# A recommendation tower: twenty embedding fields selected by one-hot matmuls, twelve gathered, in every unit

## The chip, the cores and the metric

One core of a Trainium2 chip. The metric is the device time of one execution in microseconds, for which the median of several runs is given; lower is better. A profile shows the span of one execution, a little less than its time.

## The reference, cut to what matters

2048 samples, 32 categorical fields. Each field has a table of 64 floats a row (14 tables of 1000 rows, 12 of 1250, 3 of 12500 and 3 of 125000), and each sample one row number per field.

```python
e = jnp.stack([tbl_0[ids[:, 0]], ..., tbl_31[ids[:, 31]]], axis=1)   # 2048 x 32 x 64
gram = jnp.einsum('bnd,bmd->bnm', e, e)
z = gram[:, rows, cols]                                              # the 496 pairs above the diagonal
h = jnp.concatenate([z, dense_ctx], axis=1)                          # 496 + 16 = 512
h = jnp.maximum(h @ W_top1 + b_top1, 0.0)                            # 512 -> 512
h = jnp.maximum(h @ W_top2 + b_top2, 0.0)                            # 512 -> 256
y = h @ W_top3                                                       # 256 -> 1
```

## The kernel before, in words

The batch is worked in four units of 512 samples; a unit has two rounds of 256. A row of a table reaches `vecs` (64 numbers of a field on partitions, samples and fields along them) in one of two ways.

*Gathered* fields: POOL issues one indirect DMA per field and 128 samples (`gather`, L289) into `rows`. PE transposes four fields at a time (`turn`, L502: four transposes into one half of `gat_ps`), ACT copies them to `vecs` (`gathered`, L326). The rows of a turn's slot are fetched for the next unit as soon as the turn has been made for this one: `gather(u, r, x)` waits for `gat_full` of unit u - 1. So POOL works only after turns.

*Selected* fields: the table stays in SBUF (`tabs`), split into three bf16 pieces that sum to the f32 value (ACT: `high`, `middle`; DVE: `rest` L425, `low` L430, once, during unit 0), as chunks of 125 rows: 8 chunks for 1000 rows, 10 for 1250. Two fields are a pair. SP spreads the pair's ids over all partitions (`load_wide`), DVE compares them with the row numbers (`one_hots`, L442: one instruction of 128x512 per chunk) into a ring of four pieces, PE multiplies (`select`, L487: chunks x 3 pieces x 2 fields matmuls, 48 for a pair of 8-chunk fields, 60 for 10-chunk ones), ACT copies (`selected`, L318, four copies of 64x256).

Then per round PE multiplies each sample's 32 vectors with themselves (`gram`, L517, 4 chunks of 128 small matmuls), ACT or DVE copies the products out, SP writes them to DRAM and reads them back as rows of pairs (`rows_out`, `rows_back`), and the three layers follow one unit late (L531, L540, L549), woven in between gram chunks.

PE's written order in unit u: `select(u, 2..)`, with turns of round 0 behind the later pairs; then gram of round 0 with `layer1(u-1, 0..3)`; then turns of round 1 with `select(u+1, 0)` and `select(u+1, 1)` among them; then layer 2 and 3 of u - 1 with the gram of round 1. ACT and SP have the same kind of written order. In unit 0 all gathers of both rounds are issued at once at the start.

Before the change there are 16 selected and 16 gathered fields in units 0 and 3; in units 1 and 2 (`SHIFTED`) the last pair, fields 30 and 31 (10 chunks), is gathered too, as a fifth turn of two fields. So pairs are 8, 7, 7, 8, turns per round 4, 5, 5, 4 and gathers 64, 72, 72, 64. `PAIRS`, `TURNS`, `units_with_pair`, `units_with_turn`, `turn_slots` and `turn_columns` keep account of that.

Of the kernel before, what the change touches and what calls it, by code (L numbers as in the profile page):

```python
# [13 lines left out]
P = 128  # L14
# [30 lines left out]

PAIRS = [ALL_PAIRS - (u in SHIFTED) for u in range(UNITS)]
TURNS = [ALL_TURNS - (u not in SHIFTED) for u in range(UNITS)]
PAIRS_TO = [sum(PAIRS[:u]) for u in range(UNITS + 1)]
MOST_PAIRS = max(PAIRS)
TURNS_TO = [ROUNDS * sum(TURNS[:u]) for u in range(UNITS + 1)]  # L50


def sel_no(u, g):
    return PAIRS_TO[u] + g


def gat_no(u, r, x):
    return TURNS_TO[u] + TURNS[u] * r + x


def units_with_pair(u, g):

    return sum(g < PAIRS[v] for v in range(u))


def units_with_turn(u, x):

    return sum(x < TURNS[v] for v in range(u))


def turn_slots(x):
    return slice(4 * x, min(4 * x + 4, N_ROWS))


def turn_columns(x):
    return slice(4 * x, 4 * x + 4) if 4 * x < N_GAT else slice(FIELDS - 2, FIELDS)

# [5 lines left out]
def piece_no(u, g, half, at):  # L83

    return 4 * (PAIRS_TO[u] + g) + 2 * half + at

# [6 lines left out]
def dlrm_tower_kernel(nc, chunks, ctx_t, ids_gat, ids_sel, tables, packed, w1, b1, w2, b2, w3, out):  # L93
    first_chunk = [sum(chunks[:k]) for k in range(N_SEL)]
    halves = [((0, c // 2), (c // 2, c)) for c in chunks]
    half_most = max(b - a for h in halves for a, b in h)
    pair_chunks = [(first_chunk[2 * g], chunks[2 * g] + chunks[2 * g + 1]) for g in range(ALL_PAIRS)]
    pair_most = max(k for _, k in pair_chunks)
    assert all(chunks[2 * g] == chunks[2 * g + 1] for g in range(ALL_PAIRS))

    with ExitStack() as ctx:
# [11 lines left out]
        gat_ids = sb("gat_ids", [P, UNITS * ROUNDS * 2 * N_ROWS], I32)  # L113
        sel_ids = sb("sel_ids", [P, N_SEL * BATCH // P], I32)
# [3 lines left out]
        onehot = sb("onehot", [P, RING, half_most, UNIT], BF16)  # L118
        rows = sb("rows", [P, ROUNDS, N_ROWS, 2, DIM], F32)
        vecs = sb("vecs", [P, HALF, FIELDS], F32)  # L120
# [39 lines left out]
        onehot_used = sem("onehot_used")  # L160
        rows_in = [[sem(f"rows_in{r}_{x}") for x in range(ALL_TURNS)] for r in range(ROUNDS)]
        sel_emptied = sem("sel_emptied")
# [17 lines left out]
        def _(sp):  # L180
# [7 lines left out]
            def load_wide(u, w):  # L188
                last = [v for v in range(u) if w < PAIRS[v]][-1:]
                for v in last:  # L190
                    sp.wait_ge(onehot_ready, piece_no(v, w, 1, 1) + 1)
# [38 lines left out]

            first = ROUNDS * 2 * N_ROWS
            sp.dma_start(gat_ids[:, 0:first], ids_gat[:, 0:first]).then_inc(gat_ids_in[0], 16)
# [7 lines left out]
            for w in range(N_SEL // WIDE):  # L240
                load_wide(0, w)
            for g in range(STAGE_SLOTS, MOST_PAIRS):
                load_stage(g)
# [5 lines left out]
            for u in range(LAST):  # L249
                for w in range(PAIRS[u + 1]):  # L250
# [23 lines left out]
        def _(pool):  # L274
# [8 lines left out]
            def gather(u, r, x):  # L283
                for v in [v for v in range(u) if x < TURNS[v]][-1:]:
                    pool.wait_ge(gat_full, gat_no(v, r, x) + 1)
                for k in range(N_ROWS)[turn_slots(x)]:
                    for h in range(2):
                        at = ((u * ROUNDS + r) * 2 + h) * N_ROWS + k
                        nc.gpsimd.indirect_dma_start(  # L289
                            out=rows[:, r, k, h, :], out_offset=None, in_=tables[ROWS_OF[k]],  # L290
                            in_offset=bass.IndirectOffsetOnAxis(ap=gat_ids[:, at:at + 1], axis=0))\
                          .then_inc(rows_in[r][x], 16)

            for u in range(UNITS):
                if u < 2:
                    pool.wait_ge(gat_ids_in[u], 16)
                for r in range(ROUNDS):
                    for x in range(TURNS[u]):
                        gather(u, r, x)

        @block.scalar
        def _(act):
# [19 lines left out]
            def gathered(u, r, x):  # L322
                n, at = gat_no(u, r, x), turn_columns(x)
                fields = at.stop - at.start
                act.wait_ge(gat_full, n + 1)
                nc.scalar.copy(vecs[:, P * r:P * r + P, at],  # L326
                               gat_ps[:, n % 2, 0:P * fields].rearrange("p (f j) -> p j f", f=fields))\
                  .then_inc(gat_emptied, 1)

# [45 lines left out]
            for u in range(UNITS):  # L375
                for g in range(2, PAIRS[u]):
                    selected(u, g)
                    if u == 0 and g + 4 < MOST_PAIRS:
                        high(g + 4)
                        middle(g + 4)  # L380
                    if g >= 4:
                        gathered(u, 0, g - 4)
                for x in range(PAIRS[u] - 4, TURNS[u]):
                    gathered(u, 0, x)
                if u == 0:
# [8 lines left out]
                gram(u, 0, 1, (0, 1))  # L394
                for x in range(TURNS[u]):
                    gathered(u, 1, x)
# [19 lines left out]
        def _(dve):  # L416
# [16 lines left out]
            def one_hots(u, g, half):  # L433
                if half == 0:
                    dve.wait_ge(wide_in[g], 16 * units_with_pair(u + 1, g))
                for at in range(2):
# [17 lines left out]
            rest(1)  # L454
            for g in range(MOST_PAIRS):
                one_hots(0, g, 0)
                if g + 1 < MOST_PAIRS:
                    low(g + 1)
                one_hots(0, g, 1)
                if g + 2 < MOST_PAIRS:  # L460
                    rest(g + 2)
            for u in range(1, UNITS):
                for g in range(PAIRS[u]):
# [8 lines left out]
        def _(pe):  # L472
# [22 lines left out]
            def turn(u, r, x):  # L495
                n = gat_no(u, r, x)
                if n >= 2:
                    pe.wait_ge(gat_emptied, n - 1)
                slots = range(N_ROWS)[turn_slots(x)]
                pe.wait_ge(rows_in[r][x], 16 * 2 * len(slots) * units_with_turn(u + 1, x))  # L500
                for at, k in enumerate(slots):
                    last = nc.tensor.transpose(gat_ps[:, n % 2, P * at:P * at + P],  # L502
                                               rows[:, r, k, :, :].rearrange("p h d -> p (h d)"), ident[:])
                last.then_inc(gat_full, 1)

            def gram(u, r, c):
                b = c // 2
                if c == 0:
                    pe.wait_ge(sel_emptied, PAIRS_TO[u + 1])
                    pe.wait_ge(gat_emptied, gat_no(u, r, TURNS[u] - 1) + 1)  # L510
                if c % 2 == 0 and emptied_no(u, r, b) > 0:
# [87 lines left out]
def laid_out(np, inputs):  # L599
# [18 lines left out]
    for f in SELECTED:  # L618
# [36 lines left out]
```

## Time and profile before

| | us |
|---|---|
| median of 3 runs | 666.53 (664.74 to 671.36) |
| the profiled execution | 669.14 |
| its span | 666.8 |
| PE busy (weight loads apart) | 405.4 (61%) |
| POOL busy | 267.0 (40%) |
| DVE busy | 165.0 (25%) |
| ACT busy | 142.3 (21%) |

PE is the tensor engine, PEld its weight loads, DVE the vector engine, ACT the scalar engine, POOL the engine that issues the gathers, SP the one that issues most other transfers. In a timeline the bracket is idle time ahead of the instructions and what ended it; "issue" is idle time for which the profile shows nothing awaited, "remote" one whose releaser it doesn't show. Neighbouring instructions of one kind are merged, with their count behind the x.

### The profile page before, as it was taken

The numbers are of one execution on the slowest core, as the hardware profiler recorded it, in microseconds if no ns is written. First come the engines' busy times: TensorE is split into PE (matmuls) and PEld (weight loads), VectorE is DVE, ScalarE is ACT, GpSimd is POOL, SyncE is SP. The second block draws the span as 40 slices with busy tenths as digits, with TensorE's granted clock in tenths as the row PEclk, the third lists the DMA queues.
The fourth block names the chain that finished last, engine by engine and source line by source line (L and its number), as shares of the span: only waits on it lengthen the run. The fifth ranks groups of instructions, "written<-read, shape, count | busy, mean of one in ns | idle before, by whom it ended". The sixth has DMA issues, their size and how long they took to land.

```text
span 666.8 us, 13226 instructions
## 1 busy us (share of the span) xinstructions
PE 405.4 (61%) x5956; PEld 212.2 (32%) x5956; DVE 165.0 (25%) x513; ACT 142.3 (21%) x232; POOL 267.0 (40%) x280
## 2 busy tenths in 40 slices
PE   0632138762664249641973657962793667999877
PEld 0200014321421135310530334521350234555455
DVE  4410049631022007410030203640011204720000
ACT  4020007411100033220110014340120014543111
POOL 6777700766176500675076610367047420000000
PEclk9855559955586559975995768976696669999898
DMA  8411123211011117511011004821001004501340
GB/s 274 136 28 26 28 87 131 54 22 25 9 27 23 21 27 146 148 26 22 3 25 24 17 9 74 212 61 27 6 16 26 15 12 74 114 1 20 78 93 0
DMA packets 39058, 36.08 MB, mean 54 GB/s; under 512 B 14870, under 2 KB 27992, under 8 KB 38875
## 3 DMA queue, kind: packets, MB, share of 16 engines
q1 hardware_dynamic: 29866, 25.14, 15.5%
q0 software_dynamic: 8704, 8.93, 6.8%
q8 instruction: 46, 0.75, 0.5%
q10 hardware_dynamic: 432, 1.18, 0.5%
q14 instruction: 10, 0.07, 0.0%
HBM read 27.15 MB, written 8.07 MB: 53 GB/s over the span
## 4 chain that ended last, share of the span: by engine, by line
PE 50%; issue 23%; another core or an unknown queue 13%; DVE 7%; ACT 4%; SPq 1%; DMA 1%; DVEq 0%; ACTq 0%
PE sel_ps L487 24%; PE tower_ps L531 9%; PE gram_ps L517 9%; PE tower_ps L540 5%; DVE onehot L442 4%; PE gat_ps L502 3%; ACT vecs L318 2%; PE tower_ps L549 1%; DVE work L425 1%; DVE tabs L430 1%; ACT work L335 1%; SPq L202 1%; ACT h L348 0%; DMA products<-work 0%
## 5 line engine op out<-in xcount | busy, mean ns | idle before, releaser
L289 POOL DMA_INDIRECT rows<-in_tbl_dram,gat_ids x272 | 266.1, 978 | 270.5 <-PE gat_ps L502 178.5
L487 PE MATMUL sel_ps<-onehot,tabs 128*64 128x512 bf16 x1464 | 212.9, 418 | 136.4 <-issue 83.1
L442 DVE TENSOR_SCALAR onehot<-ids_wide,row_ids 128x512 bf16<-128x512 f16 x488 | 141.0, 361 | 324.1 <-PE sel_ps L487 183.4
L487 PEld LDWEIGHTS sel_ps<-onehot,tabs 128*64 128x64 bf16 x1464 | 93.1, 118 | 248.5 <-issue 174.2
L517 PE MATMUL gram_ps<-vecs 64*32 64x32 f32 x4096 | 62.7, 215 | 106.2 <-issue 95.4
L318 ACT COPY vecs<-sel_ps 64x256 f32<-64x256 f32 x120 | 72.1, 601 | 100.1 <-PE sel_ps L487 58.5
L517 PEld LDWEIGHTS gram_ps<-vecs 64*32 64x32 f32 x4096 | 50.4, 116 | 133.1 <-issue 121.2
L531 PE MATMUL tower_ps<-work,w_sb 128*128 128x512 f32 (+1 forms) x160 | 67.9, 580 | 2.8 <-DMA work<-products 2.8
L531 PEld LDWEIGHTS tower_ps<-work,w_sb 128*128 128x128 f32 x160 | 34.0, 221 | 27.5 <-issue 21.2
L326 ACT COPY vecs<-gat_ps 128x512 f32<-128x512 f32 (+1 forms) x36 | 19.7, 567 | 107.3 <-remote 45.1
L449 DVE COPY work<-gram_ps 128x512 f32<-128x512 f32 x8 | 5.2, 687 | 135.4 <-PE gram_ps L517 135.4
L540 PE MATMUL tower_ps<-h,w_sb 128*128 128x512 f32 (+1 forms) x80 | 35.4, 596 | 1.1 <-ACT h L341 1.1
L341 ACT ACTIVATE h<-tower_ps,b_sb 128x512 f32<-128x512 f32 (+1 forms) x20 | 12.0, 602 | 96.8 <-PE tower_ps L531 78.0
L502 PE MATMUL gat_ps<-ident,rows 128*128 128x128 f32 x136 | 23.7, 311 | 11.0 <-issue 10.4
L311 ACT CAST tabs<-work 128x1024 bf16<-128x1024 f32 (+1 forms) x8 | 8.6, 1072 | 86.5 <-DVE work L425 65.5
L335 ACT COPY work<-gram_ps 128x512 f32<-128x512 f32 x24 | 13.0, 589 | 50.0 <-PE gram_ps L517 50.0
L502 PEld LDWEIGHTS gat_ps<-ident,rows 128*128 128x128 f32 x136 | 16.4, 156 | 21.8 <-issue 20.7
L540 PEld LDWEIGHTS tower_ps<-h,w_sb 128*128 128x128 f32 x80 | 17.1, 223 | 15.2 <-issue 12.4
L348 ACT ACTIVATE h<-tower_ps,b_sb 128x512 f32<-128x512 f32 (+1 forms) x10 | 5.5, 599 | 59.2 <-PE tower_ps L540 59.2
L425 DVE TENSOR_TENSOR work<-work,tabs 128x1024 f32<-128x1024 f32 (+1 forms) x8 | 10.1, 1262 | 4.3 <-issue 4.3
L430 DVE TENSOR_TENSOR tabs<-work,tabs 128x1024 bf16<-128x1024 f32 (+1 forms) x8 | 10.1, 1267 | 1.1 <-issue 1.1
L549 PE MATMUL tower_ps<-h,w_sb 128*1 128x512 f32 (+1 forms) x20 | 9.1, 582 | 1.9 <-ACT h L348 1.9
(12 smaller groups left out, 15.1 us busy)
## 6 DMA issues: line engine op xcount, KB each, us to landing
ids_wide<-ids_scratch SPq DMA_DIRECT2D x30, 256.0 KB
rows<-in_tbl_dram,gat_ids POOLq DMA_INDIRECT x272
products<-work SPq DMA_DIRECT2D x12, 248.0 KB, 4.2
products<-work SPq DMA_DIRECT2D x24, 120.0 KB, 4.5
work<-in_packed_dram SPq DMA_DIRECT2D x5, 512.0 KB
work<-products SPq DMA_DIRECT2D x9, 256.0 KB
work<-in_packed_dram ACTq DMA_DIRECT2D x2, 512.0 KB
w_sb<-in_w_dram SPq DMA_DIRECT2D x1, 1024.0 KB, 6.0
```

Source lines behind the costliest of these rows:

```text
L289: nc.gpsimd.indirect_dma_start(out=rows[:, r, k, h, :], out_offset=None, in_=tables[ROWS_OF[k]], in_offset=bass.IndirectOffsetOnAxis(ap=ga ...
L318: last = nc.scalar.copy(vecs[DIM * h:DIM * h + DIM, :, N_GAT + 2 * g + at], sel_ps[DIM * at:DIM * at + DIM, sel_no(u, g) % 2, HALF * h:HAL ...
L326: nc.scalar.copy(vecs[:, P * r:P * r + P, at], gat_ps[:, n % 2, 0:P * fields].rearrange("p (f j) -> p j f", f=fields))\
L335: nc.scalar.copy(gram_rows[:, r, h, :, 16 * b:16 * b + 16], gram_ps[:, h, :, :].rearrange("p i m -> p m i")).then_inc(gram_emptied, 1)
L425: nc.vector.tensor_tensor(piece, piece, tabs[:, c0:c0 + k, 0, :], ALU.subtract).then_inc(rest_ready, 1)
L430: nc.vector.tensor_tensor(tabs[:, c0:c0 + k, 2, :], stage[g % STAGE_SLOTS][:, 0:k, :], tabs[:, c0:c0 + k, 1, :], ALU.subtract).then_inc(ta ...
L442: last = nc.vector.tensor_scalar(onehot[:, n % RING, c - c0, :], ids_wide[:, k, :], row_ids[chunks[k]][:, c:c + 1], None, ALU.is_equal)
L487: last[at] = nc.tensor.matmul(sel_ps[DIM * at:DIM * at + DIM, n % 2, :], tabs[:, first_chunk[k] + c, part, :], onehot[:, piece_no(u, g, ha ...
L502: last = nc.tensor.transpose(gat_ps[:, n % 2, P * at:P * at + P], rows[:, r, k, :, :].rearrange("p h d -> p (h d)"), ident[:])
L517: last = nc.tensor.matmul(gram_ps[32 * s:32 * s + 32, h, i, :], v, v, start=True, stop=True, skip_group_check=True)
L531: last = nc.tensor.matmul(tower_ps[:, j % 2, 0:width], w1_sb[:, c, P * j:P * j + P], z[:, c, x0:x0 + width], start=(c == 0), stop=(c == Q ...
L540: last = nc.tensor.matmul(tower_ps[:, o, 0:width], w2_sb[:, j, P * o:P * o + P], h1[:, j, 0:width], start=(j == 0), stop=(j == J1 - 1), sk ...
```

## The change

Fields 16, 21, 23 and 29 (1250 rows each) join the selected ones. All units then have ten pairs (seven of 8 chunks, then three of 10) and three turns of four gathered fields per round, and the accounting of units that differ goes. The last pairs are [27, 28] of 8 chunks and [16, 21], [23, 29], [30, 31] of 10. `tabs` grows from 132 to 172 chunks, `ids_wide` from 16 to 20 fields, `rows` shrinks from 18 to 12 fields. A turn of round 0 now follows pair 7, 8 and 9 (it followed pairs 4 to 7, and more behind them); in round 1 nothing is left after the third turn. The table laid out for `packed`, the rows of the first layer's weights (`ORDER`) and the ids follow the new lists.

```diff
-SELECTED = [7, 8, 9, 11, 12, 15, 17, 18, 20, 22, 24, 25, 27, 28, 30, 31]
+SELECTED = [7, 8, 9, 11, 12, 15, 17, 18, 20, 22, 24, 25, 27, 28, 16, 21, 23, 29, 30, 31]
 GATHERED = [f for f in range(FIELDS) if f not in SELECTED]
 ORDER = GATHERED + SELECTED
 N_SEL, N_GAT = len(SELECTED), len(GATHERED)
-
-SHIFTED = (1, 2)
-ROWS_OF = GATHERED + SELECTED[-2:]
-N_ROWS = len(ROWS_OF)
-ALL_PAIRS, ALL_TURNS = N_SEL // 2, N_GAT // 4 + 1
+N_PAIRS, N_TURNS = N_SEL // 2, N_GAT // 4
...
-PAIRS = [ALL_PAIRS - (u in SHIFTED) for u in range(UNITS)]
-TURNS = [ALL_TURNS - (u not in SHIFTED) for u in range(UNITS)]
-PAIRS_TO = [sum(PAIRS[:u]) for u in range(UNITS + 1)]
-MOST_PAIRS = max(PAIRS)
-TURNS_TO = [ROUNDS * sum(TURNS[:u]) for u in range(UNITS + 1)]
...
             def gather(u, r, x):
-                for v in [v for v in range(u) if x < TURNS[v]][-1:]:
-                    pool.wait_ge(gat_full, gat_no(v, r, x) + 1)
-                for k in range(N_ROWS)[turn_slots(x)]:
+                if u > 0:
+                    pool.wait_ge(gat_full, gat_no(u - 1, r, x) + 1)
+                for k in range(4 * x, 4 * x + 4):
                     for h in range(2):
...
             for u in range(UNITS):
-                for g in range(2, PAIRS[u]):
+                for g in range(2, N_PAIRS):
                     selected(u, g)
-                    if u == 0 and g + 4 < MOST_PAIRS:
+                    if u == 0 and g + 4 < N_PAIRS:
                         high(g + 4)
                         middle(g + 4)
-                    if g >= 4:
-                        gathered(u, 0, g - 4)
-                for x in range(PAIRS[u] - 4, TURNS[u]):
-                    gathered(u, 0, x)
+                    if g >= N_PAIRS - N_TURNS:
+                        gathered(u, 0, g - N_PAIRS + N_TURNS)
...
             for u in range(UNITS):
-                for g in range(2, PAIRS[u]):
+                for g in range(2, N_PAIRS):
                     select(u, g)
-                    if g >= 4:
-                        turn(u, 0, g - 4)
-                for x in range(PAIRS[u] - 4, TURNS[u]):
-                    turn(u, 0, x)
+                    if g >= N_PAIRS - N_TURNS:
+                        turn(u, 0, g - N_PAIRS + N_TURNS)
...
                 turn(u, 1, 2)
                 if u < LAST:
                     select(u + 1, 1)
-                for x in range(3, TURNS[u]):
-                    turn(u, 1, x)
                 if u > 0:
                     layer2(u - 1, 0)
                 gram(u, 1, 0)
```

## Rows read from the trace of the kernel before

**Rows 1.** The page's 40 slices of the span, busy tenths and granted clock:
```profile
PE   0632138762664249641973657962793667999877
...
POOL 6777700766176500675076610367047420000000
PEclk9855559955586559975995768976696669999898
```

**Rows 2.** The chain of waits, its longest piece (start, length, what):
```profile
36.54 54.24 another core or an unknown queue
```

**Rows 3.** The page's groups: busy, mean ns of one, idle before and releaser:
```profile
L289 POOL DMA_INDIRECT rows<-in_tbl_dram,gat_ids x272 | 266.1, 978 | 270.5 <-PE gat_ps L502 178.5
L487 PE MATMUL sel_ps<-onehot,tabs 128*64 128x512 bf16 x1464 | 212.9, 418 | 136.4 <-issue 83.1
L442 DVE TENSOR_SCALAR onehot<-ids_wide,row_ids 128x512 bf16<-128x512 f16 x488 | 141.0, 361 | 324.1 <-PE sel_ps L487 183.4
...
L425 DVE TENSOR_TENSOR work<-work,tabs 128x1024 f32<-128x1024 f32 (+1 forms) x8 | 10.1, 1262 | 4.3 <-issue 4.3
```

**Rows 4.** The timeline of POOL (start, busy, what, idle before):
```profile
3.29 1.18 POOL L289 DMA_INDIRECT rows<-in_tbl_dram,gat_ids  x1 [1.83 <-DMA gat_ids<-in_ids_gat_dram]
...
83.96 0.94 POOL L289 DMA_INDIRECT rows<-in_tbl_dram,gat_ids  x1 [0.30 <-issue]
115.89 3.80 POOL L289 DMA_INDIRECT rows<-in_tbl_dram,gat_ids  x1 [30.99 <-PE gat_ps L502]
...
166.97 0.94 POOL L289 DMA_INDIRECT rows<-in_tbl_dram,gat_ids  x1 [0.30 <-issue]
...
203.64 0.94 POOL L289 DMA_INDIRECT rows<-in_tbl_dram,gat_ids  x1 [3.10 <-remote]
...
311.37 0.94 POOL L289 DMA_INDIRECT rows<-in_tbl_dram,gat_ids  x1 [0.30 <-issue]
...
370.67 2.89 POOL L289 DMA_INDIRECT rows<-in_tbl_dram,gat_ids  x1 [6.49 <-PE gat_ps L502]
```

**Rows 5.** The timeline of PE, from 59 us to the last unit:
```profile
59.29 0.59 PE L487 MATMUL sel_ps<-onehot,tabs 128*64 128x512 bf16 x1 [2.21 <-issue]
...
94.20 7.30 PE L487 MATMUL sel_ps<-onehot,tabs 128*64 128x512 bf16 x48 [17.52 <-DVE onehot L442]
...
114.46 0.66 PE L502 MATMUL gat_ps<-ident,rows 128*128 128x128 f32 x4
...
179.47 1.97 PE L502 MATMUL gat_ps<-ident,rows 128*128 128x128 f32 x8
...
202.67 4.77 PE L487 MATMUL sel_ps<-onehot,tabs 128*64 128x512 bf16 x19 [1.46 <-issue]
...
246.65 18.30 PE L487 MATMUL sel_ps<-onehot,tabs 128*64 128x512 bf16 x144 [2.45 <-ACT vecs L318]
...
265.46 5.37 PE L487 MATMUL sel_ps<-onehot,tabs 128*64 128x512 bf16 x48
...
316.94 1.18 PE L517 MATMUL gram_ps<-vecs 64*32 64x32 f32 x91 [0.49 <-issue]
...
333.56 1.09 PE L502 MATMUL gat_ps<-ident,rows 128*128 128x128 f32 x8
...
369.28 1.54 PE L502 MATMUL gat_ps<-ident,rows 128*128 128x128 f32 x6
...
389.89 6.28 PE L540 MATMUL tower_ps<-h,w_sb 128*128 128x512 f32 x8
...
407.79 17.46 PE L487 MATMUL sel_ps<-onehot,tabs 128*64 128x512 bf16 x144 [2.49 <-ACT vecs L318]
...
557.43 15.80 PE L487 MATMUL sel_ps<-onehot,tabs 128*64 128x512 bf16 x144 [2.55 <-ACT vecs L318]
...
585.52 6.67 PE L487 MATMUL sel_ps<-onehot,tabs 128*64 128x512 bf16 x60
```

**Rows 6.** The timeline of DVE, where it resumes after the first gathers:
```profile
90.88 1.14 DVE L442 TENSOR_SCALAR onehot<-ids_wide,row_ids 128x512 bf16<-128x512 f16 x4 [54.34 <-remote]
```

More of the change, by code:

```diff
@@ L43 @@
 MOVES = 3 * Q
-PAIRS = [ALL_PAIRS - (u in SHIFTED) for u in range(UNITS)]
-TURNS = [ALL_TURNS - (u not in SHIFTED) for u in range(UNITS)]
-PAIRS_TO = [sum(PAIRS[:u]) for u in range(UNITS + 1)]
-MOST_PAIRS = max(PAIRS)
-TURNS_TO = [ROUNDS * sum(TURNS[:u]) for u in range(UNITS + 1)]
 def sel_no(u, g):
-    return PAIRS_TO[u] + g
+    return N_PAIRS * u + g
 def gat_no(u, r, x):
[L58 to L76, printed above, removed]
+    return N_TURNS * (ROUNDS * u + r) + x
 def emptied_no(u, r, b):
@@ L83, in piece_no @@
 def piece_no(u, g, half, at):
-    return 4 * (PAIRS_TO[u] + g) + 2 * half + at
+    return 4 * (N_PAIRS * u + g) + 2 * half + at
 def pair_row(n, m):
@@ L96, in dlrm_tower_kernel @@
     half_most = max(b - a for h in halves for a, b in h)
-    pair_chunks = [(first_chunk[2 * g], chunks[2 * g] + chunks[2 * g + 1]) for g in range(ALL_PAIRS)]
+    pair_chunks = [(first_chunk[2 * g], chunks[2 * g] + chunks[2 * g + 1]) for g in range(N_PAIRS)]
     pair_most = max(k for _, k in pair_chunks)
-    assert all(chunks[2 * g] == chunks[2 * g + 1] for g in range(ALL_PAIRS))
+    assert all(chunks[2 * g] == chunks[2 * g + 1] for g in range(N_PAIRS))
     with ExitStack() as ctx:
@@ L118, in dlrm_tower_kernel @@
         onehot = sb("onehot", [P, RING, half_most, UNIT], BF16)
-        rows = sb("rows", [P, ROUNDS, N_ROWS, 2, DIM], F32)
+        rows = sb("rows", [P, ROUNDS, N_GAT, 2, DIM], F32)
         vecs = sb("vecs", [P, HALF, FIELDS], F32)
@@ L160, in dlrm_tower_kernel @@
         onehot_used = sem("onehot_used")
-        rows_in = [[sem(f"rows_in{r}_{x}") for x in range(ALL_TURNS)] for r in range(ROUNDS)]
+        rows_in = [[sem(f"rows_in{r}_{x}") for x in range(N_TURNS)] for r in range(ROUNDS)]
         sel_emptied = sem("sel_emptied")
@@ L188, in load_wide @@
             def load_wide(u, w):
-                last = [v for v in range(u) if w < PAIRS[v]][-1:]
-                for v in last:
-                    sp.wait_ge(onehot_ready, piece_no(v, w, 1, 1) + 1)
+                if u > 0:
+                    sp.wait_ge(onehot_ready, piece_no(u - 1, w, 1, 1) + 1)
                 sp.dma_start(ids_wide[:, WIDE * w:WIDE * w + WIDE, :],
@@ L229, in store @@
                   .then_inc(y_out[v % 2], 16)
-            first = ROUNDS * 2 * N_ROWS
+            first = ROUNDS * 2 * N_GAT
             sp.dma_start(gat_ids[:, 0:first], ids_gat[:, 0:first]).then_inc(gat_ids_in[0], 16)
@@ L241, in _ @@
                 load_wide(0, w)
-            for g in range(STAGE_SLOTS, MOST_PAIRS):
+            for g in range(STAGE_SLOTS, N_PAIRS):
                 load_stage(g)
@@ L249, in _ @@
             for u in range(LAST):
-                for w in range(PAIRS[u + 1]):
+                for w in range(N_PAIRS):
                     load_wide(u + 1, w)
@@ L283, in gather @@
             def gather(u, r, x):
-                for v in [v for v in range(u) if x < TURNS[v]][-1:]:
-                    pool.wait_ge(gat_full, gat_no(v, r, x) + 1)
-                for k in range(N_ROWS)[turn_slots(x)]:
+                if u > 0:
+                    pool.wait_ge(gat_full, gat_no(u - 1, r, x) + 1)
+                for k in range(4 * x, 4 * x + 4):
                     for h in range(2):
-                        at = ((u * ROUNDS + r) * 2 + h) * N_ROWS + k
+                        at = ((u * ROUNDS + r) * 2 + h) * N_GAT + k
                         nc.gpsimd.indirect_dma_start(
-                            out=rows[:, r, k, h, :], out_offset=None, in_=tables[ROWS_OF[k]],
+                            out=rows[:, r, k, h, :], out_offset=None, in_=tables[GATHERED[k]],
                             in_offset=bass.IndirectOffsetOnAxis(ap=gat_ids[:, at:at + 1], axis=0))\
@@ L297, in _ @@
                 for r in range(ROUNDS):
-                    for x in range(TURNS[u]):
+                    for x in range(N_TURNS):
                         gather(u, r, x)
@@ L322, in gathered @@
             def gathered(u, r, x):
-                n, at = gat_no(u, r, x), turn_columns(x)
-                fields = at.stop - at.start
+                n = gat_no(u, r, x)
                 act.wait_ge(gat_full, n + 1)
-                nc.scalar.copy(vecs[:, P * r:P * r + P, at],
-                               gat_ps[:, n % 2, 0:P * fields].rearrange("p (f j) -> p j f", f=fields))\
-                  .then_inc(gat_emptied, 1)
+                nc.scalar.copy(vecs[:, P * r:P * r + P, 4 * x:4 * x + 4],
+                               gat_ps[:, n % 2, :].rearrange("p (f j) -> p j f", f=4)).then_inc(gat_emptied, 1)
             def gram(u, r, b, halves):
@@ L394, in _ @@
                 gram(u, 0, 1, (0, 1))
-                for x in range(TURNS[u]):
+                for x in range(N_TURNS):
                     gathered(u, 1, x)
@@ L434, in one_hots @@
                 if half == 0:
[L435 removed]
+                    dve.wait_ge(wide_in[g], 16 * (u + 1))
                 for at in range(2):
@@ L454, in _ @@
             rest(1)
-            for g in range(MOST_PAIRS):
+            for g in range(N_PAIRS):
                 one_hots(0, g, 0)
-                if g + 1 < MOST_PAIRS:
+                if g + 1 < N_PAIRS:
                     low(g + 1)
                 one_hots(0, g, 1)
-                if g + 2 < MOST_PAIRS:
+                if g + 2 < N_PAIRS:
                     rest(g + 2)
             for u in range(1, UNITS):
-                for g in range(PAIRS[u]):
+                for g in range(N_PAIRS):
                     one_hots(u, g, 0)
@@ L498, in turn @@
                     pe.wait_ge(gat_emptied, n - 1)
-                slots = range(N_ROWS)[turn_slots(x)]
-                pe.wait_ge(rows_in[r][x], 16 * 2 * len(slots) * units_with_turn(u + 1, x))
-                for at, k in enumerate(slots):
+                pe.wait_ge(rows_in[r][x], 16 * 2 * 4 * (u + 1))
+                for at in range(4):
                     last = nc.tensor.transpose(gat_ps[:, n % 2, P * at:P * at + P],
-                                               rows[:, r, k, :, :].rearrange("p h d -> p (h d)"), ident[:])
+                                               rows[:, r, 4 * x + at, :, :].rearrange("p h d -> p (h d)"), ident[:])
                 last.then_inc(gat_full, 1)
@@ L508, in gram @@
                 if c == 0:
-                    pe.wait_ge(sel_emptied, PAIRS_TO[u + 1])
-                    pe.wait_ge(gat_emptied, gat_no(u, r, TURNS[u] - 1) + 1)
+                    pe.wait_ge(sel_emptied, N_PAIRS * (u + 1))
+                    pe.wait_ge(gat_emptied, gat_no(u, r, N_TURNS - 1) + 1)
                 if c % 2 == 0 and emptied_no(u, r, b) > 0:
@@ L623, in laid_out @@
         "ctx_t": given["dense_ctx"].T,
-        "ids_gat": ids[..., ROWS_OF].transpose(3, 4, 0, 2, 1, 5).reshape(P, -1),
+        "ids_gat": ids[..., GATHERED].transpose(3, 4, 0, 2, 1, 5).reshape(P, -1),
         "ids_sel": ids[..., SELECTED].transpose(0, 5, 1, 2, 3, 4).reshape(P, -1),
-        **{f"tbl_{f}": given[f"tbl_{f}"] for f in ROWS_OF},
+        **{f"tbl_{f}": given[f"tbl_{f}"] for f in GATHERED},
         "packed": packed,
@@ L648 @@
     out = nc.dram_tensor("out_0_dram", (BATCH, 1), _mybir.dt.float32, kind="ExternalOutput").ap()
-    tables = {f: args[f"tbl_{f}"] for f in ROWS_OF}
+    tables = {f: args[f"tbl_{f}"] for f in GATHERED}
     chunks = [inputs[f"tbl_{f}"].shape[0] // KROWS for f in SELECTED]
```

2 lines of the change are left out of this document (1 added, 1 removed).

## The prediction

> **What bounds the kernel now.** I read the slices of the page first, then the chain of waits, then the timelines of POOL, PE and DVE side by side. In the slices the rows of PE and POOL are nearly each other's negative: in the first slice of a stretch of POOL work PE is mostly still at 6 or 7 tenths, then it falls to 1 to 4, and where POOL is at 0 PE is mostly at 7 to 9 [rows 1]. The chain's longest single piece is 54.24 us at 36.54 in which nothing on this core's compute engines works [rows 2]. The timelines say what it is. POOL issues the first unit's 64 gathers from 3.29 to 84.90 [rows 4]; PE, in the middle of its second `select`, puts out one matmul every 2.8 us (0.59 busy, 2.21 "issue") [rows 5], and DVE, whose wait has no late partner in the profile ("remote", 54.34 us), moves again at 90.88, 6 us after the last gather [rows 6]. PE is back at 94.20 [rows 5]. It repeats in each later run of gathers: gathers until 312.31, PE back at speed at 316.94; a second, short run starts at 370.67, and PE is back at 389.89 [rows 4, 5]. I call such a run a burst: PE keeps its pace for one slice at its start, then only trickles until 5 to 9 us after its last gather. Gathers come at a pitch of 1.25 us (0.94 and 0.30 of issue) [rows 4]: 272 of them make 340 us, and all matmuls of the selection at their best pace (48 in 5.37 us, 0.112 each [rows 5]) make 164. So POOL's gathers are the largest term, PE outside them the second; DVE with 141 us of one-hots [rows 3] leads only in the first unit, where it also splits the tables.
>
> **What the change does to the counts.** A unit gathers 12 fields in 3 turns per round: 2 x 12 x 2 = 48 gathers in place of 64, 72, 72 and 64, so 192 in place of 272 (-80, or -100 us of bursts at 1.25). A unit selects 10 pairs, the last three of ten chunks (60 matmuls each), in place of 8, 7, 7, 8: 2064 matmuls in place of 1464 (+600, or +67 us at 0.112; one such pair is 6.67 us against 5.37 [rows 5]). Turns go from 36 to 24; a turn is 0.66 [rows 5]. The bare balance is -100 + 67 - 7 = -40. What the stages let through of it, unit by unit, from boundaries in [rows 5] (94.20, 114.46, 179.47, 246.65 for unit 0; 265.46, 333.56, 369.28, 407.79 for unit 1; 557.43 for the start of unit 3's selects):
>
> **Unit 0, start.** 48 gathers in place of 64: 16 x 1.25 = -20.0. Everything hangs on the last gather, so PE resumes at 74 in place of 94.2. The two added broadcasts of ids and the larger tables are on queues that have long been done or that wait for DVE; I cost them at nothing because the burst covers them. Uncovered they would be 0.5 MB, some 3 us.
>
> **Unit 0, selects ahead of the first turn.** The first turn comes after pair 7, not after pair 4: three pairs more lie outside any burst. Here DVE sets the pace: one-hots at 0.285 each (1.14 for 4 [rows 6]), splits at 1.26 [rows 3], some 1.5 for ten chunks (an estimate by size). Check on an old pair: 16 x 0.28 + 2 x 1.26 = 7.0, and from 94.20 to the end of the first turn three pairs took 20.9. New: 52 x 0.28 + 1.26 + 5 x 1.5 = +23.3. ACT's longer coupling (it splits up to pair 9) has 4 to 5 us per pair and is hidden.
>
> **Unit 0, the two bursts.** Each has 24 gathers in place of 36 (the first from 115.89 to 167.91, the second in two parts around a pause of 3.10 us before 203.64 [rows 4]): 2 x 12 x 1.25 = -30.0. Unit 0 in all: -20.0 + 23.3 - 30.0 = -26.7.
>
> **Unit 1.** Three more pairs ahead of the first turn, at PE's pace: 5.37 + 5.37 + 6.67 = +17.4. Round 0's burst loses 12 gathers, -15.0, but the two pairs beside it are the long ones, 2 x 1.3: -12.4. In round 1 the burst of 24 stays as it is (turns 0, 1 and 2 release it just as now), but the second burst, released by the turns 3 and 4, goes: from 369.28 to 389.89 PE did two turns, half of layer 2 and one gram chunk in 20.6 us [rows 5]; without it they are 3.9 + 1.6 = 5.5 (an estimate from the matmuls' undisturbed pace), -15.1. What is late next there is PE itself. With less idling ahead of it the next unit's selects start at the higher of the clock's two levels: 144 matmuls take 15.80 where PE has worked steadily and 18.30 and 17.46 where not [rows 5], so -2.5. Sum: -12.6.
>
> **Unit 2.** +17.4; its bursts fetch for unit 3, which had 64, so round 0 loses 8 gathers (-10.0 + 2.6 = -7.4), and the second burst of round 1 had 8 gathers, not 12 (-15.1 + 5.0 = -10.1); clock -1.7. Sum: -1.8.
>
> **Unit 3.** No gathers at all; PE is the bound. Two more pairs of 6.67 are +13.3, two turns fewer -1.3: +12.0. Nothing covers this.
>
> **Sum:** -26.7 - 12.6 - 1.8 + 12.0 = -29.1. The profiled execution took 669.14 around a span of 666.8 (2.3 us outside it, unchanged): 637.7 + 2.3 = 640.0. The median of the runs is 666.53, 2.6 below that execution, so I forecast 637. The removed waits for a turn's slot and the planner functions that go cost nothing either way: the same kinds of waits stay, one per turn.
>
> Bounds of what the trace doesn't show. An added matmul costs 0.112 at best and 0.251 where PE crawls (19 in 4.77 us [rows 5]); most of the added ones lie ahead of the first turn, outside bursts, so I take the first. A removed gather is worth 1.25 if the stall ends with the burst, which three places show, and less only if the pause returns elsewhere. PE's stretches of layer 2 may speed up too (6.28 for 8 matmuls at 389.89 against 3.7 to 3.9 warm): up to 2.6 for each of units 1 and 2, not in the sum.
>
> **Why gathers should matter to PE at all.** The trace shows the coincidence, not the wire: slow issue within every burst, full pace outside [rows 1, 4, 5]. The Trainium skill says otherwise: "SBUF — State Buffer", section "SBUF: two separate sides", holds that DMAs and compute engines use separate ports, that only VectorE and GpSimd share a pair, and that PE and ACT never wait on anyone. By that rule the gathers would take nothing from PE and their removal would give nothing (the first rival); the trace (2.21 us idle per matmul while only gathers run) speaks against it.
>
> **Rivals.**
> - *The gathers only coincide with the stalls* (what throttles PE is tied to its own stream, so the stalls stay). Then nothing of the -100 comes, and the kernel pays 67 - 7 = +60: 727. Against it: PE recovers each time within 5 to 9 us of the last gather. 2%. The Trainium skill's page on SBUF named above would have it so.
> - *The added matmuls run crawling.* The decision lies where 600 x p - 107 = 0, p = 0.178 us. At 0.251, if the clock stays at its lower level in the longer selects and trickling eats them, it is +44: 711. For it: PEclk is 5 in 11 of the 40 slices [rows 1]; against it: 144 matmuls after a stall take 18.30, 0.127 each, and the 48 of the fourth pair 5.37 again [rows 5]. 5%.
> - *Signals are lost anew.* In round 0 only three turns release the gathers, and turn 2 comes some 17 us after turn 0, inside the burst. If POOL doesn't see it until the burst has drained, it pauses 3 us as at 203.64, and DVE and ACT with it 6 us, then a new burst of 8 begins in the gram: 9 x 3 rounds less what PE gets done in the pause, +20: 657. 13%.
> - *All is let through*: the bare balance of -40, with warm layers and clock -5 to -10 more: 616 to 627. For it: a pause in POOL is also free time for PE. 15%.
> - *The change does nothing measurable*: unit 0's selects at DVE's pace and the pauses eat it; 6%.
>
> **How the numbers follow.** Forecast 637 with 628 to 650 around it: 59%. With the fourth rival below it (15%) and the third up to 660 (13%) the range 617 to 660 holds some 85% if the terms are sized rightly, and the 8 in 10 wanted with what their sizing can miss by. A difference under 1% (6.7 us) could not be told from none here. Faster by over 1%: forecast, third and fourth rival, 87%; within 1%: 6%; slower: 7%.
>
> **What would show it.** Right: 192 gathers and 2064 matmuls of the selection; the first burst over at about 65 and PE back near 74; the first turn near 117; unit 1's selects starting near 220 in place of 246.65; a single burst per round, none after the turns of round 1 but one of 24; unit 3's stretch from its selects to the end 12 us longer than 109. Wrong: a PE that is back later than 9 us after a burst, pauses in POOL with "remote" in round 0 of each unit, or a mean of a selection matmul above 0.15 outside bursts. The prediction fails most easily on unit 0, where 27 of the 29 us arise and where DVE, ACT and PE are locked to each other.

## The result, and the profile after

The changed kernel takes 627.0 us (median of 4 runs, 625.8 to 627.2) against 665.8 for the kernel before beside it: ratio 0.939, 95% interval 0.934 to 0.944, 39 us less. Forecast were 637 and 29 us less.

The page of the changed kernel: slices of the span and the groups that answer to [rows 1, 3].

```profile
PE   0722487953845699749836799857945889999877
...
POOL 6777100454472000660571000661373000000000
PEclk9955599985665599987966999986965789999798
...
L453 PE MATMUL sel_ps<-onehot,tabs 128*64 128x512 bf16 x2064 | 279.8, 404 | 119.5 <-issue 73.1
L408 DVE TENSOR_SCALAR onehot<-ids_wide,row_ids 128x512 bf16<-128x512 f16 x688 | 196.7, 360 | 275.3 <-PE sel_ps L453 146.5
L259 POOL DMA_INDIRECT rows<-in_tbl_dram,gat_ids x192 | 184.5, 961 | 289.1 <-PE gat_ps L467 220.4
```

The counts are the forecast ones, 192 gathers and 2064 matmuls. The clock is higher: PEclk is 5 in 7 slices, not 11. The timeline of PE gives the boundaries of the stages, as [rows 5] did.

```profile
68.27 0.58 PE L453 MATMUL sel_ps<-onehot,tabs 128*64 128x512 bf16 x1 [1.51 <-issue]
...
73.55 7.22 PE L453 MATMUL sel_ps<-onehot,tabs 128*64 128x512 bf16 x48 [2.54 <-DVE onehot L408]
...
115.55 0.66 PE L467 MATMUL gat_ps<-ident,rows 128*128 128x128 f32 x4
...
161.20 1.97 PE L467 MATMUL gat_ps<-ident,rows 128*128 128x128 f32 x8
...
212.50 28.53 PE L453 MATMUL sel_ps<-onehot,tabs 128*64 128x512 bf16 x240 [2.45 <-ACT vecs L288]
...
247.98 0.66 PE L467 MATMUL gat_ps<-ident,rows 128*128 128x128 f32 x4
...
301.19 1.09 PE L467 MATMUL gat_ps<-ident,rows 128*128 128x128 f32 x8
...
356.40 27.88 PE L453 MATMUL sel_ps<-onehot,tabs 128*64 128x512 bf16 x240 [2.45 <-ACT vecs L288]
...
503.06 27.86 PE L453 MATMUL sel_ps<-onehot,tabs 128*64 128x512 bf16 x240 [2.44 <-ACT vecs L288]
```

Stage by stage, in us. The 114.46 and 247.98 turns count to their ends; the end of the span is 666.8 before and 625.4 after. The spans are those of the profiled executions; that of before is 2.6 us above its median, so the spans differ by 41.4 us and the medians by 38.8.

| stage | before | after | change | forecast |
|---|---|---|---|---|
| unit 0, until PE is back | 94.2 | 73.6 | -20.6 | -20.0 |
| unit 0, selects to the first turn | 20.9 | 42.7 | +21.7 | +23.3 |
| unit 0, round 0 | 64.4 | 45.0 | -19.4 | -15.0 |
| unit 0, round 1 | 67.2 | 51.3 | -15.9 | -15.0 |
| unit 1, selects to the first turn | 18.8 | 36.1 | +17.3 | +14.9 |
| unit 1, round 0 | 68.1 | 52.6 | -15.5 | -12.4 |
| unit 1, round 1 | 74.2 | 55.2 | -19.0 | -15.1 |
| unit 2 | 149.6 | 146.7 | -3.0 | -1.8 |
| unit 3 | 109.4 | 122.3 | +13.0 | +12.0 |
| sum | 666.8 | 625.4 | -41.4 | -29.1 |

POOL's timeline of the changed kernel shows the pauses that a rival foresaw. In unit 1 as in units 0 and 2, round 0's 24 gathers come as three groups of eight with a "remote" wait between.

```profile
248.91 1.11 POOL L259 DMA_INDIRECT rows<-in_tbl_dram,gat_ids  x1 [55.97 <-PE gat_ps L467]
...
260.63 0.94 POOL L259 DMA_INDIRECT rows<-in_tbl_dram,gat_ids  x1 [1.86 <-remote]
...
272.34 0.95 POOL L259 DMA_INDIRECT rows<-in_tbl_dram,gat_ids  x1 [2.02 <-remote]
```

The kernel before has such pauses in round 0 too. It makes two in unit 0, so that its 36 gathers come as 16, 8 and 12, and one in each of units 1 and 2 (8 and 28, 8 and 24):

```profile
141.55 0.95 POOL L289 DMA_INDIRECT rows<-in_tbl_dram,gat_ids  x1 [2.99 <-remote]
...
153.25 0.94 POOL L289 DMA_INDIRECT rows<-in_tbl_dram,gat_ids  x1 [2.01 <-remote]
...
277.54 0.95 POOL L289 DMA_INDIRECT rows<-in_tbl_dram,gat_ids  x1 [1.67 <-remote]
...
437.79 1.07 POOL L289 DMA_INDIRECT rows<-in_tbl_dram,gat_ids  x1 [1.83 <-remote]
```

So the change adds no pause in unit 0 and one each in units 1 and 2, and on balance they did not cost time: round 0 gained 3 to 4 us more per unit than my sum has. That was the first question for the experiments: is it each gather that costs, or a long row of them?

### The profile page after: what moved, and what is told of

Same layout as the page of the kernel before. It is cut to its first block, busy times and chain, and to the rows that moved or that the text cites. A ratio compares the mean times of both kernels' runs of the same rounds, so it can differ in the third digit from the quotient of the medians.

```text
span 625.4 us, 14522 instructions
## 1 busy us (share of the span) xinstructions
PE 450.0 (72%) x6516; PEld 237.0 (38%) x6516; DVE 225.9 (36%) x717; ACT 165.9 (27%) x264; POOL 185.4 (30%) x200
## 4 chain that ended last, share of the span: by engine, by line
PE 53%; issue 16%; another core or an unknown queue 10%; DVE 9%; ACT 7%; DMA 2%; SPq 1%; ACTq 0%; DVEq 0%
PE sel_ps L453 30%; PE tower_ps L496 8%; PE gram_ps L482 8%; DVE onehot L408 6%; ACT vecs L288 5%; PE tower_ps L505 5%; PE tower_ps L514 2%; DVE tabs L396 1%; PE gat_ps L467 1%; DVE work L391 1%; DMA work<-in_packed_dram 1%; ACT work L303 1%; ACT vecs L295 1%; SPq L174 1%
## 5 line engine op out<-in xcount | busy, mean ns | idle before, releaser
L453 PE MATMUL sel_ps<-onehot,tabs 128*64 128x512 bf16 x2064 | 279.8, 404 | 119.5 <-issue 73.1
L408 DVE TENSOR_SCALAR onehot<-ids_wide,row_ids 128x512 bf16<-128x512 f16 x688 | 196.7, 360 | 275.3 <-PE sel_ps L453 146.5
L259 POOL DMA_INDIRECT rows<-in_tbl_dram,gat_ids x192 | 184.5, 961 | 289.1 <-PE gat_ps L467 220.4
L453 PEld LDWEIGHTS sel_ps<-onehot,tabs 128*64 128x64 bf16 x2064 | 132.1, 115 | 260.3 <-issue 155.7
L288 ACT COPY vecs<-sel_ps 64x256 f32<-64x256 f32 x160 | 96.6, 604 | 131.1 <-PE sel_ps L453 69.2
L482 PE MATMUL gram_ps<-vecs 64*32 64x32 f32 x4096 | 51.9, 218 | 48.0 <-issue 26.5
L482 PEld LDWEIGHTS gram_ps<-vecs 64*32 64x32 f32 x4096 | 44.9, 118 | 71.4 <-issue 47.3
L295 ACT COPY vecs<-gat_ps 128x512 f32<-128x512 f32 x24 | 13.8, 592 | 49.5 <-remote 33.6
L467 PE MATMUL gat_ps<-ident,rows 128*128 128x128 f32 x96 | 15.7, 296 | 0.6 <-ACT vecs L295 0.6
L467 PEld LDWEIGHTS gat_ps<-ident,rows 128*128 128x128 f32 x96 | 10.8, 147 | 7.2 <-issue 6.2
```

The source lines that it names most:

```text
L259: nc.gpsimd.indirect_dma_start(out=rows[:, r, k, h, :], out_offset=None, in_=tables[GATHERED[k]], in_offset=bass.IndirectOffsetOnAxis(ap=g ...
L288: last = nc.scalar.copy(vecs[DIM * h:DIM * h + DIM, :, N_GAT + 2 * g + at], sel_ps[DIM * at:DIM * at + DIM, sel_no(u, g) % 2, HALF * h:HAL ...
L295: nc.scalar.copy(vecs[:, P * r:P * r + P, 4 * x:4 * x + 4], gat_ps[:, n % 2, :].rearrange("p (f j) -> p j f", f=4)).then_inc(gat_emptied, 1)
L408: last = nc.vector.tensor_scalar(onehot[:, n % RING, c - c0, :], ids_wide[:, k, :], row_ids[chunks[k]][:, c:c + 1], None, ALU.is_equal)
L453: last[at] = nc.tensor.matmul(sel_ps[DIM * at:DIM * at + DIM, n % 2, :], tabs[:, first_chunk[k] + c, part, :], onehot[:, piece_no(u, g, ha ...
L482: last = nc.tensor.matmul(gram_ps[32 * s:32 * s + 32, h, i, :], v, v, start=True, stop=True, skip_group_check=True)
```

## The experiments

### First four: a chip on which nothing stalls

`e_land_after` puts a wait on POOL behind the eight gathers of a turn, for their landing:

```diff
             def gather(u, r, x):
...
                           .then_inc(rows_in[r][x], 16)
+                pool.wait_ge(rows_in[r][x], 16 * 8 * (u + 1))
```

> The kernel after, with one wait more on POOL: behind each turn's eight gathers it waits until they have landed, so that no more than eight are ever in a row. Theory A (what stalls the other engines is a long unbroken run of gathers; eight in a row with a pause behind them cost PE almost nothing, as round 0 of units 1 and 2 of the changed kernel hints): faster, 575 to 605 us, and PE makes progress with its selects in the first 70 us. Theory B (every gather costs PE 1.25 us wherever it stands, as the prediction's sum had it): the pauses give nothing, 622 to 645 us.

`e_one_unit` leaves out the gathers of units 1 to 3:

```diff
-            for u in range(UNITS):
+            for u in range(1):
                 if u < 2:
                     pool.wait_ge(gat_ids_in[u], 16)
...
-                pe.wait_ge(rows_in[r][x], 16 * 2 * 4 * (u + 1))
+                pe.wait_ge(rows_in[r][x], 16 * 2 * 4)
```

> The kernel after, with the gathers of units 1 to 3 left out (144 of 192; the turns transpose the rows of unit 0 again), all other work the same. If gathers stall PE: units 1 and 2 fall from 144 and 147 us to the pace of the last unit, some 103 us, and unit 0 loses about 45 us, 490 to 520 us in all. If the stalls belong to PE's own stream and only coincide with the gathers: 620 to 630 us.

`e_unshift` is the kernel before with one line changed:

```diff
-SHIFTED = (1, 2)
+SHIFTED = ()
```

> The kernel before with SHIFTED empty: all units eight pairs and four turns, 256 gathers for 272 and 1584 selection matmuls for 1464. A small step of the same kind as the change. Balance at 1.25 us a gather and 0.112 us a matmul: -20 + 13.4 - 2 = -9, 657 us (650 to 661). If the gain of the change comes from the burst's form and not from its length (fewer turns per round, three in place of four or five): 666 to 680 us, since here four turns stay.

`e_land_before` is the kernel before with the same kind of wait as the first:

```diff
+                pool.wait_ge(rows_in[r][x], 16 * 2 * len(range(N_ROWS)[turn_slots(x)]) * units_with_turn(u + 1, x))
```

> The kernel before with the same wait for landing behind each turn's gathers. Theory A: faster than before by at least as much as in the kernel after, since there are more and longer runs: 600 to 640 us. Theory B: 665 to 690 us.

Measured: `e_land_after` 469.5 (459.5 to 470.4), `e_one_unit` 456.9, `e_unshift` 421.4 (415.6 to 426.2), `e_land_before` 473.1. None of these can be set against 666 or 627, because **the kernel before, run beside them, took 412.2 us** (409.3 to 417.8 in 7 runs). By that time it was not the chip of the result, or not in its condition. All four expectations are void in their numbers: they took the stall for a property of the program.

The same stretch, 20 to 66 us, in the first burst of both conditions (busy us and counts of PE, PEld, DVE, ACT, POOL, granted clock, DMA share, GB/s). First the kernel before on the chip of the result:

```profile
20.00:66.00 46.00, 15.44 (x70) 4.84 (x66) 7.07 (x18) 5.28 (x7) 35.03 (x37) 0.61 0.19 41
```

then `e_unshift`, which differs from it in this stretch by nothing, on the other chip:

```profile
20.00:66.00 46.00, 35.43 (x310) 17.36 (x308) 45.64 (x113) 25.83 (x36) 34.83 (x37) 1.00 0.43 128
```

POOL does the same in both, 37 gathers in 35 us. PE puts out 70 matmuls in one and 310 in the other, DVE 18 instructions and 113. So gathers and stall can be parted: it takes the gathers and that chip (or its condition at the time). What a kernel without stalls is bound by can be read in the second row: DVE is busy 45.6 of the 46 us of this part of unit 0, and PE is its follower.

`e_land_before` is 61 us slower than the kernel before there. It is no test of theory A, which has no stall to remove there, but it shows what the waits can cost. With 32 or 36 gathers a round and pauses between them POOL becomes late, and PE waits for rows, as its timeline shows:

```profile
107.15 1.09 PE L503 MATMUL gat_ps<-ident,rows 128*128 128x128 f32 x4 [4.51 <-DMA rows<-in_tbl_dram,gat_ids]
```

### Two on a chip that stalls

`r_after` is the kernel after, unchanged; `r_land_after` is `e_land_after` again.

> The kernel after, unchanged, beside the kernel before on the chip of this call. In the first four experiments the kernel before took 412 us, not 666, with the same instructions and the same pitch of its gathers, so the stalls during gathers belong to the chip or its condition, not to the program. Where the kernel before takes about 412: the removed gathers are worth nothing and the 600 added matmuls of the selection cost 0.112 us or DVE's pace, less the turns, 412 + 67 - 7 = 472, or 455 to 475 with the 457 us of the variant without later gathers as the nearest row; so slower by 10 to 15 per cent. Where it takes about 666: 625 to 629 as in the result.

> The kernel after with POOL waiting for each turn's eight gathers to land. Where the kernel before takes about 666 us: theory A (unbroken runs of gathers stall PE) 575 to 605 us; theory B (every gather costs 1.25 us) 622 to 645 us. Where it takes about 412 us: as measured in the first experiments, 465 to 472 us, no less than the kernel after.

Here the kernel before took 667.1 (665.0 to 678.1). `r_after`: 630.6, ratio 0.940 (0.932 to 0.949), the result again. `r_land_after`: **586.8, ratio 0.880 (0.872 to 0.889)**, 44 us faster than the kernel after beside it, with all of its work and all of its gathers, and waits added. Theory A's forecast (575 to 605) came, theory B (622 to 645, the form that my sum used) falls. Its first burst in the same stretch:

```profile
20.00:66.00 46.00, 34.17 (x262) 17.08 (x260) 38.48 (x98) 21.14 (x29) 29.11 (x28) 0.89 0.50 153
```

28 gathers in place of 36, but 262 matmuls in place of the 66 of the kernel after (50 in `r_after` beside it). PE's first turn comes at 82 in place of 116. POOL's timeline shows what the pauses are, 2 to 6 us until the landing:

```profile
20.24 0.94 POOL L259 DMA_INDIRECT rows<-in_tbl_dram,gat_ids  x1 [5.83 <-DMA rows<-in_tbl_dram,gat_ids]
...
32.63 0.94 POOL L259 DMA_INDIRECT rows<-in_tbl_dram,gat_ids  x1 [1.91 <-DMA rows<-in_tbl_dram,gat_ids]
...
44.40 0.94 POOL L259 DMA_INDIRECT rows<-in_tbl_dram,gat_ids  x1 [1.74 <-DMA rows<-in_tbl_dram,gat_ids]
```

The pauses do not merely give PE a window of 2 us each. While the group of 20.24 to 30.7 runs, PE works at 24 matmuls in 2.78 us, 0.116 each, its pace outside bursts:

```profile
22.70 2.78 PE L454 MATMUL sel_ps<-onehot,tabs 128*64 128x512 bf16 x24 [0.19 <-issue]
26.16 2.78 PE L454 MATMUL sel_ps<-onehot,tabs 128*64 128x512 bf16 x24 [0.69 <-DVE onehot L409]
```

It is no full cure: later in unit 0 the gram still trickles, from 105 to 124, beside two groups of eight with their waits (101.06 to 110.8 and 112.58 to 122.3). So an unbroken run of more than eight is not what it takes to hold up the gram; the selects are what the groups set free.

```profile
108.30 0.32 PE L483 MATMUL gram_ps<-vecs 64*32 64x32 f32 x4 [1.11 <-issue]
109.73 0.33 PE L483 MATMUL gram_ps<-vecs 64*32 64x32 f32 x3 [1.12 <-issue]
```

Of the 160 us that the kernel after takes more on this chip than on the others (below), the pauses return 44.

### Six more, all on chips without stalls

`p_one_unit`, `q_one_unit` and `s_one_unit` are `e_one_unit` again. `q_after` is the kernel after again. `p_land4` waits after every four gathers:

```diff
                           .then_inc(rows_in[r][x], 16)
+                    if k % 2 == 1:
+                        pool.wait_ge(rows_in[r][x], 16 * (8 * u + 2 * (k - 4 * x) + 2))
```

`p_plain_pool` reads the first 128 rows of each table, without the ids:

```diff
-                        nc.gpsimd.indirect_dma_start(
-                            out=rows[:, r, k, h, :], out_offset=None, in_=tables[GATHERED[k]],
-                            in_offset=bass.IndirectOffsetOnAxis(ap=gat_ids[:, at:at + 1], axis=0))\
+                        nc.gpsimd.dma_start(rows[:, r, k, h, :], tables[GATHERED[k]][0:P, :])\
                           .then_inc(rows_in[r][x], 16)
```

> The kernel after with the gathers of units 1 to 3 left out (144 of 192). On a chip where the kernel before takes about 666 us: if the gathers stall PE, 500 to 530 us, with the first 48 gathers' stall left in it; if the stall is PE's own, 620 to 630. On a chip where it takes about 412: 455 to 460, as measured before. The difference between the two chips must then be the first burst alone, 40 to 60 us.

> The kernel after with POOL waiting for the landing of every four gathers instead of eight. On the chip with 666 us for the kernel before: if it is the queue of unfinished gathers that stalls the others, even shorter runs remove more of it, 530 to 575 us against the 587 of the waits by eight; if the pauses only give PE a window of 2 us per group, it comes with the lengthening of the gathers' time (48 pauses of about 3 us each), 575 to 600. On the chip with 412 us: 480 to 520, since PE then waits for rows.

> The kernel after with every gather replaced by a plain transfer of the same size and shape from POOL's queue (the first 128 rows of the table; the ids are left out). If the stall comes with POOL's software-written transfers as such: 600 to 640 us on the chip with 666 us for the kernel before. If it takes the reading of the ids or the scattered rows of 256 bytes: below 520 us.

> The kernel after, unchanged, once more beside the kernel before. On a chip where the kernel before takes about 412 us: 455 to 462 us, 10 to 12 per cent slower, since leaving 144 of its gathers out gave 457 and 458 us there and the removed gathers are then covered anyway. On a chip with 666 us for the kernel before: 625 to 631 as measured twice.

> The kernel after with the gathers of units 1 to 3 left out. With 666 us for the kernel before: 500 to 530 us if the gathers stall PE, 620 to 630 if the stall is PE's own. With 412 us: within 5 us of the kernel after beside it, that is the gathers of units 1 to 3 cost nothing there.

> The kernel after with the gathers of units 1 to 3 left out, in the hope of the chip on which gathers stall. With 666 us for the kernel before: 500 to 530 us if the gathers stall PE (the first burst of 48 is left), 620 to 630 if the stall is PE's own. With 412 us: 457 to 460 as before.

| run | us | before beside it | ratio, 95% interval |
|---|---|---|---|
| `q_after` | 467.4 | 411.6 | 1.139 (1.133 to 1.145) |
| `q_one_unit` | 459.4 | 411.6 | 1.115 (1.104 to 1.126) |
| `p_one_unit` | 458.2 | 412.0 | 1.116 (1.106 to 1.126) |
| `s_one_unit` | 458.3 | 412.9 | 1.107 (1.098 to 1.115) |
| `p_land4` | 467.5 | 412.0 | 1.137 (1.126 to 1.147) |
| `p_plain_pool` | 453.6 | 412.0 | 1.103 (1.094 to 1.112) |

**The change is 14% slower where nothing stalls.** 467.4 lies above my 455 to 462 (and inside the 455 to 475 with 472 as the bare balance of the expectation of `r_after`). The gathers of units 1 to 3 cost 8 us there (459.4 against 467.4), more than the 5 that I allowed; the page shows them in the gram, whose 4096 matmuls are busy 53.3 us with the gathers beside them and 43.8 without (first row `q_after`, then, beside it on the same chip with the gathers left out, `q_one_unit`):

```profile
L482 PE MATMUL gram_ps<-vecs 64*32 64x32 f32 x4096 | 53.3, 210 | 19.5 <-issue 9.3
```
```profile
L482 PE MATMUL gram_ps<-vecs 64*32 64x32 f32 x4096 | 43.8, 207 | 21.3 <-issue 13.1
```

`p_land4` is a miss too: I expected 480 to 520, since PE would wait for rows; 24 gathers a round leave POOL enough room, and the pauses cost nothing. `p_plain_pool` gains 14 us over `q_after`, partly since DVE's one-hots take 348 ns in place of 366; it says nothing on the stall, for which it was meant. Its gram is busy 43.7 us, as without gathers, though the same number of transfers leaves POOL's queue; since one takes POOL 0.56 us in place of 0.97, their bursts are also shorter, and the two were not told apart. What `e_one_unit` would take on the stalling chip was not measured.

`q_after` by its timeline of PE, the boundaries at which units 1, 2 and 3 start their selects:

```profile
137.25 27.71 PE L453 MATMUL sel_ps<-onehot,tabs 128*64 128x512 bf16 x240 [2.45 <-ACT vecs L288]
...
241.01 26.19 PE L453 MATMUL sel_ps<-onehot,tabs 128*64 128x512 bf16 x240 [2.45 <-ACT vecs L288]
...
343.30 26.19 PE L453 MATMUL sel_ps<-onehot,tabs 128*64 128x512 bf16 x240 [2.45 <-ACT vecs L288]
```

The units take 137.3, 103.8, 102.3 and 119.8 us, on the stalling chip 212.5, 143.9, 146.7 and 122.3. The last unit, which gathers nothing, is nearly alike; the stall sits in the three others, 75, 40 and 44 us. The 240 matmuls of five pairs take 26.2 to 27.7 against 27.9 to 28.5. With the stall the granted clock is lower as well (0.83 to 0.84 in the runs of the result, 0.94 to 0.95 in those of `q_after`), so the difference holds also what idling costs through the clock; it was not taken apart.

## Why the prediction was right, and where it was off

**The balance.** Two kernels on two kinds of chip part it into work and stall:

| | stalling chip | others | difference |
|---|---|---|---|
| before, 272 gathers | 665.8 | 411.6 | 254.2 |
| after, 192 gathers | 627.0 | 467.4 | 159.6 |
| change | -38.8 | +55.8 | -94.6 |

The work added costs 56 us net, where the bare balance said 67 - 7 = 60. The stall removed is 95, where it said 100. So the two large terms and the sign are right, and for the reason given: on that chip gathers hold up PE, and the change trades them for matmuls. That the difference between chips is the stall rests on the timelines, in which PE's pace outside bursts is nearly the same, and on the last unit.

That 95 is so near to 100 is partly luck. At 1.25 a gather the stall would be 340 us before and 240 after; measured are 254 and 160, or 0.93 and 0.83 a gather. Both are too high by 80 to 86 us, and in the difference that cancels.

**The signs named.** Came: the counts, the first burst over at 65.4, PE back at 73.6, its first turn done at 116.2, unit 3 longer by 13. Missed: unit 1's selects start at 212.5, not near 220, and round 0's burst is not a single one. One sign of being wrong appeared, the "remote" pauses in round 0 of each unit. It could not decide anything: the kernel before has them as well, which I had overlooked.

**Unit 0, start**: -20.6 for -20.0. DVE was back at 71 and PE at 73.6, forecast "near 74". The uncovered price of the larger tables did not show.

**Selects ahead of the first turn**: +21.7 for +23.3, set by DVE as said; its 10-chunk splits take 1.48, taken at 1.5.

**The step that was mis-sized** is "Round 0's burst loses 12 gathers, -15.0" with its likes: the bursts of round 0 gave -19.4, -15.5 and -10.9 where the sum had -15.0, -12.4 and -7.4, together 11 us; the whole sum missed by 12, and its other misses nearly cancel. It priced a removed gather at 1.25 and nothing else. The timelines give what the bursts took, from POOL's first gather to the end of its last, and then until PE is back at pace, in us:

| round 0 of unit | POOL's burst, before, after | change (1.25 a gather) | from its end until PE is back |
|---|---|---|---|
| 0 | 52.0, 33.2 | -18.8 (-15.0) | 2.2, 1.5 |
| 1 | 46.5, 33.1 | -13.4 (-15.0) | 4.6, 1.5 |
| 2 | 41.5, 33.2 | -8.3 (-10.0) | 4.0, 1.5 |

PE's return is at 170.14, 316.94 [rows 5] and 471.62 before, at 151.77, 283.57 and 426.84 after. Three of these rows, of unit 0 before, then of units 0 and 2 after:

```profile
170.14 2.13 PE L517 MATMUL gram_ps<-vecs 64*32 64x32 f32 x181 [0.49 <-issue]
```
```profile
151.77 2.19 PE L482 MATMUL gram_ps<-vecs 64*32 64x32 f32 x188 [1.08 <-issue]
...
426.84 0.87 PE L482 MATMUL gram_ps<-vecs 64*32 64x32 f32 x61 [1.11 <-issue]
```

In unit 0 the excess is in the burst itself: the kernel before had one gather of 3.80 [rows 4] and a pause of 2.99 in it, where after they are 1.07 and 1.98. In units 1 and 2 the added pause costs about 2 us, and more than that comes back in two places. The long pairs, summed as +2.6, run beside the burst and add nothing, and PE is back 1.5 us after the last gather in place of 4.6 and 4.0. The last unbroken run of gathers is 8 long after the change, 28 and 24 before it, and 12 in unit 0, where PE took 2.2 us.

That the form of the burst matters to the selects shows in one program run twice. In unit 0 the result's kernel made its round 0 gathers as 8, 8 and 8, and the round took 45.0 us; `r_after` made them as 16 and 8, its pair 9 trickled beside the 16, POOL then waited 6.98 us for the late turn, and the round took 50.6 (115.9 to 166.4):

```profile
145.38 0.95 POOL L259 DMA_INDIRECT rows<-in_tbl_dram,gat_ids  x1 [6.98 <-PE gat_ps L467]
```

In the result's run PE gets through pairs 8 and 9 beside the first two groups of eight (busy 8.9 and 7.0 us of 9.8 and 9.7); beside the third the gram trickles (2.4 of 9.8), as in `r_land_after`.

**Unit 1, round 1**: -19.0 for -15.1. The second burst went as forecast (6.3 us for half of layer 2 and a gram chunk, forecast 5.5). The other half of layer 2 takes 3.70 where it took 6.28 [rows 5], the 2.6 us that I had named and not summed, and the rest of the gram with layer 3 takes 9.2 where it took 11.7, which I had not named. **The clock in the selects**: -2.5 and -1.7 were forecast, and hardly any of it came. The two added pairs at 5.37 make 29.0 and 28.2 us of the old 18.30 and 17.46; measured for the 240 matmuls are 28.53 and 27.88, so -0.5 and -0.3. **Unit 3**: +13.0 for +12.0.

**The rivals.** *All is let through*, at 15%, gave 616 to 627, by the bare balance 626.5, and was nearest; I had its arithmetic and preferred the stages' own sum. *Signals are lost anew* was right that POOL would pause in round 0 of each unit, and wrong in sign: the pauses cost about 2 us each, and PE works on at pace in the selects beside them. *The gathers only coincide*: the same gathers at the same pitch leave PE alone on three chips, so the rival has a point that I did not see. They are no sufficient cause. It is refuted on the chip of `r_after`, which stalls as that of the result does: there POOL's waits alone changed the time by 44 us. By the Trainium skill ("SBUF — State Buffer", section "SBUF: two separate sides") PE never waits on anyone; on the chips without stalls the trace agrees as far as PE's pace in the selects goes (310 matmuls in 46 us beside 37 gathers), on the other PE issues 70 in that time. The trace shows idle time ahead of issue there and not at which port or queue it arises, so it does not show that what the Trainium skill states of the ports is wrong. *Added matmuls crawling*: did not come; the 240 of five pairs take 0.116 to 0.119 each on the stalling chip, and later pairs 0.111 to 0.112.

**Not foreseen** in any part: that the baseline itself is 412 us on other chips, and the change 56 us slower there. No chip was met in both conditions, so whether it is the chip or what it was in at the time stays open. The profile of before had the sign of it: a stall in which nothing in the program is awaited. I read it as a property of gathers.

## What to carry to other kernels

Where a profile shows long "issue" and "remote" time that no wait of the program explains, run the unchanged kernel on a second chip before tuning around it: this change is 6% faster in one condition and 14% slower in the other. Where gathers do stall the core, break their run first: a wait for landing behind every eight gained 44 us there. Without the stall such waits cost nothing measurable with 192 gathers (469.5 behind every eight, 467.5 behind every four, 467.4 without), but 61 us with 272, where POOL had no slack. Of the versions tried, the changed kernel with that wait is the fastest on the stalling chip (587), and the kernel before on the others (412).

## What the runs showed of the hardware

- One chip, or two alike, of those used took 1.6 times as long for the kernel before (666 and 667 us) as three others (412 to 413), with the same durations of gathers (0.94 to 0.95 us, pitch 1.25). In the long first burst there a selection matmul comes about every 2.8 us, other engines' waits end late, and PE is back at pace 1.5 us after the last gather where the last unbroken run was 8 long, and 9 us after it where it was 64. What sets that chip apart, or what state it was in, and by which path gathers reach PE, DVE and ACT there, stays open: no run here could tell.
- Where PE trickles, its rows in the timeline start near multiples of 0.7 us apart: 0.7 and 1.4 in the gram (276.44, 277.15, 277.86, 279.28), 1.4, 2.1 and 2.8 in the selects (63.37, 66.17, 68.27, 69.67), both in the kernel after.
- On chips without the stall gathers still slow the gram of 64x32 matmuls (53.3 against 43.8 us busy).
